# Four layer programs of a graph network joined into one, with weights split at each boundary and the undirected scores computed in strips

## The reference

```python
for layer in (undirected, attention1, attention2, directed):
    h = relu(layernorm(x)); x = x + layer(h)
# undirected, twice:
m_left, m_right = h @ Wl.T, h @ Wr.T
u_left, u_right = h @ m_left.T / sqrt(384), h @ m_right.T / sqrt(384)
u = u_left * (upper triangle and diagonal of adj) + u_right * (upper triangle of adj).T
e = exp(u) * adj; a = e / (e.sum(2) + 1e-10)
h = relu(layer_norm(a @ (h @ Wlin.T + b)) * gain + beta)
# attention
s = q @ k.T * scale + bias; p = softmax(s); out = (p @ v) @ Wo.T + bo
# directed, twice: softmax(h @ h.T / sqrt(384)) * adj, normalised, then three products
# (above, on and below the diagonal) with three weight matrices, layer norm, relu
```

## Time and profile before

| | |
|---|---|
| median of 3 runs | 3056.74 us (3055.41 to 3057.33) |
| the profiled execution | 3056.15 us |
| its span in the trace | 3054.4 us |
| mean granted TensorE clock | 0.983 |
| TensorE busy | 2807.4 us (92%) |
| VectorE, POOL, ScalarE busy | 2043.4 (67%), 1311.5 (43%), 1214.8 us (40%) |

### The profile page before, as it was taken

The page is one execution under the profiler, slowest core; times in us unless marked ns, Lnnn a source line. Parts: engine busy times, 40 slices in busy tenths (PEclk is TensorE's granted clock), DMA queues, the critical chain, the costliest instruction groups (busy, mean ns, idle before and its releaser), DMA issues. The chain is left out here.

```text
span 3054.4 us, 82121 instructions
## 1 busy us (share of the span) xinstructions
PE 2807.4 (92%) x32768; PEld 2576.5 (84%) x32768; DVE 2043.4 (67%) x3932; ACT 1214.8 (40%) x1941; POOL 1311.5 (43%) x2315
## 2 busy tenths in 40 slices
PE   6999999999968999999879999999699999999997
PEld 6888888888868888888768888888588888888886
DVE  4666666666656777777657777777567777777776
ACT  3333333333333333333333333333345454545443
POOL 1212222221213333333323333333267878878787
PEclk9999999999989999999989999999799999999999
DMA  4111111111121111111121111111211111112120
GB/s 137 39 63 50 57 57 57 57 38 61 52 84 37 45 45 45 45 45 45 45 66 46 44 45 44 45 44 47 77 32 46 52 52 52 52 35 68 34 69 31
DMA packets 116482, 158.81 MB, mean 52 GB/s; under 512 B 8000, under 2 KB 112320, under 8 KB 116416
## 3 DMA queue, kind: packets, MB, share of 16 engines
q1 hardware_dynamic: 116416, 157.88, 16.0%
HBM read 107.52 MB, written 50.33 MB: 52 GB/s over the span
## 5 line engine op out<-in xcount | busy, mean ns | idle before, releaser
L162 PE MATMUL ps<-t_hi,w_hi 128*128 128x256 f32 x2304 | 662.7, 288 | 51.7 <-DVE t_lo L900 49.1
L164 PE MATMUL ps<-t_hi,w_lo 128*128 128x256 f32 x2304 | 647.8, 281 | 0.0
L163 PE MATMUL ps<-t_lo,w_hi 128*128 128x256 f32 x2304 | 647.1, 281 | 0.0
L162 PE MATMUL ps<-w_hi,t_hi 128*128 128x384 f32 x1536 | 534.9, 348 | 3.7 <-ACT q L845 3.6
L164 PE MATMUL ps<-w_hi,t_lo 128*128 128x384 f32 x1536 | 517.7, 337 | 0.0
L163 PE MATMUL ps<-w_lo,t_hi 128*128 128x384 f32 x1536 | 517.6, 337 | 0.0
L162 PEld LDWEIGHTS ps<-t_hi,w_hi 128*128 128x128 f32 x2304 | 436.7, 190 | 83.2 <-DVE t_lo L900 58.2
L163 PEld LDWEIGHTS ps<-t_lo,w_hi 128*128 128x128 f32 x2304 | 437.0, 190 | 0.0
L164 PEld LDWEIGHTS ps<-t_hi,w_lo 128*128 128x128 f32 x2304 | 436.7, 190 | 0.0
L814 POOL TENSOR_TENSOR e<-e,factor 128x512 f32<-128x512 f32 x192 | 195.1, 1043 | 448.6 <-DVE factor L938 448.6
L1196 POOL TENSOR_TENSOR hw<-hw,w_row 128x192 f32<-128x192 f32 x512 | 348.1, 711 | 53.8 <-ACT hw L1277 52.3
(11 more groups left out here) (150 smaller groups left out, 6272.9 us busy)
## 6 DMA issues: line engine op xcount, KB each, us to landing
x_after<-xout SPq DMA_DIRECT2D x96, 384.0 KB, 2.5
xin<-x_after SPq DMA_DIRECT2D x96, 384.0 KB, 3.4
xin<-in_x SPq DMA_DIRECT2D x32, 384.0 KB, 4.2
x<-in_x SPq DMA_DIRECT2D x32, 384.0 KB, 3.6
x<-x_after SPq DMA_DIRECT2D x32, 384.0 KB, 3.6
out<-xout SPq DMA_DIRECT2D x32, 384.0 KB, 2.8
w_raw<-in_w SPq DMA_DIRECT2D x4, 2304.0 KB, 8.8
adjin<-in_adj SPq DMA_DIRECT2D x32, 256.0 KB, 3.7
```

What stands on the lines that cost most here:

```text
L162: nc.tensor.matmul(out, lhs_hi, rhs_hi, start=(k == 0), stop=False)
L163: nc.tensor.matmul(out, lhs_hi, rhs_lo, start=False, stop=False)
L164: last = nc.tensor.matmul(out, lhs_lo, rhs_hi, start=False, stop=(k == len(terms) - 1))
```

## The change

There is now one program for all four phases, without a barrier between them. `run` issues, on each engine, the first round of phase 0, then for each phase its round 1 and its loop (`run_middle`), and between two phases a line of the new table `BETWEEN` (`run_between`), in which primed stages are the last ones of the old phase, unprimed stages the first ones of the new, and `w2` is the split of matrix 2. Waits count on the old phase's semaphores where a buffer was used by it.

```diff
+SLOTS = ((0, 1, 2, 3, 4, 5), (0, 1, 2, 3), (4, 5, 0, 1), (2, 3, 4, 5, 0, 1))
+PRESPLIT = {1: (), 2: (0, 1), 3: (0, 1)}
+BETWEEN = [
...
+        "aT_0.1' z_0.1' ml_1.0' hT_1.1' mr_1.0' soft_1.0' aT_1.0' ml_1.1' mr_1.1' z_1.0' soft_1.1' aT_1.1' "
+        "z_1.1' w0 w1 w2 w3 norm.0 hT.0 q.0 norm.1 k.0 hT.1 q.1",
...
+        "stat.0 pv.0' hT.0 soft.1' out.0' stat.1 fac.1' w2 w3 v.0 pv.1' hT.1 soft.0 out.1' fac.0 v.1",
...
+        "pv.0' soft.1' out.0' fac.1' pv.1' out.1' w2 w3 w4 w5 stat.0 stat.1 split_0.0 soft_0.0 att_0.0 "
...
+def run_between(line, ended, begun):
+    for word in line.split():
+        if word[0] == "w" and word[1:].isdigit():
+            begun["weights"](int(word[1:]))
+            continue
+        stage, s = word.rstrip("'").rsplit(".", 1)
+        if word.endswith("'"):
+            ended[stage](int(s), ITER - 1)
+        else:
+            begun[stage](int(s), 0)
...
+def weights_free(eng, phases, phase, m):
+    for past in (phase - 1, phase - 2):
+        if past >= 0 and SLOTS[phase][m] in SLOTS[past]:
+            user = phases[past].weight_users[SLOTS[past].index(SLOTS[phase][m])]
+            for s in range(STREAMS):
+                eng.wait_ge(phases[past].pe_done[s], phases[past].PE[s](user, ITER - 1))
+            return
...
+        def run(eng, k, weights=None):
...
+            run_first(phases[0].orders[k], todo[0])
+            for n, ph in enumerate(phases):
+                def meanwhile(to=n + 1):
+                    if weights:
+                        for m in PRESPLIT[to]:
+                            weights(to, m)
+                run_middle(eng, ph.orders[k], todo[n], meanwhile if n + 1 < len(phases) else None)
+                if n + 1 < len(phases):
+                    run_between(BETWEEN[n][k], todo[n], todo[n + 1])
+            run_last(phases[-1].orders[k], todo[-1])
```

```diff
-                                at = t * P + half * NODES
-                                mm = nc.tensor.matmul(
-                                    b.ps[t * NODES:(t + 1) * NODES, 2 - 2 * l, half * P:(half + 1) * P],
-                                    b.hT[:, c, at:at + NODES], b.mlr[:, c, :, at:at + NODES],
-                                    start=(c == 0), stop=(c == C - 1))
+                            for blk in range(2):
+                                first_token = t * P + half * NODES + blk * HD
+                                to = t * NODES + blk * HD
+                                wanted = slice(blk * HD, blk * HD + 3 * HD)
+                                mm = nc.tensor.matmul(
+                                    b.ps[to:to + HD, 2 - 2 * l, half * P:(half + 1) * P][:, wanted],
+                                    b.hT[:, c, first_token:first_token + HD],
+                                    b.mlr[:, c * T * 2 + t * 2 + half].rearrange("p k j -> p (k j)")[:, wanted],
+                                    start=(c == 0), stop=(c == C - 1), tile_position=(0, to))
```

## The result

The changed kernel took 3013.07 us (median of 4 runs, 3009.77 to 3014.13) against 3057.03 for the kernel before on the same chip: ratio 0.9854 [0.9838, 0.987], 44 us less. The forecast was 3017 in 2998 to 3038.

What follows compares the result with a forecast made beforehand. TensorE's work was taken to bound the phases, the wait that ends last the boundaries. Terms -19.5 + 0 - 20.4 - 8.4 + 8 + 1 = -39.3 from 3056.15 gave 3017 us, range 2998 to 3038.

Steps and rivals of the forecast that it cites:

- boundary 2 to 3: Between phases 2 and 3: first idle time stays, TensorE's second, 6.43 us, goes with 2.5 of clock; -8.4 us (-12 to -5).
- boundary 1 to 2: Between phases 1 and 2: of 32.6 us over the steady distances, 12.2 remain; -20.4 us (-16 to -26.5).
- the two presplits: After round 1 of phases 1 and 2: early splits delay VectorE's softmax and POOL's products; +8 us for both (0 to +12).
- the start: Phase 0's matrices 4 and 5 load some 5 us later, first used in the second layer; +1 us (0 to 2).
- boundary 0 to 1: Between phases 0 and 1: barrier (3.0) and slow POOL pair (1.9) out, four splits (5.2) in; 0 us (-1 to +2).
- The strips: Scores `u` of phase 0: 96 instead of 128 columns, stage 1.53 to 1.225 us, 64 stages; -19.5 us.
- Downstream waits are counted from `u`'s end, so the gain stays: Step of the strips term in phase 0: the whole 0.305 us per stage is kept, 64 times, -19.5 us.
- The load rule: Skill's rule for `u`: loads overlap matmuls only in another row group, so 24 extra loads are exposed; prediction took them as hidden.
- The rival of two strips abreast: Rival for `u`: only two strips run abreast, 24 rounds of 96 columns, stage 2.2 us, +43, kernel 3079 us; chance 0.06.
- The wait at `v`: Boundary 1 to 2: `v`'s product waits for VectorE's splits `w2 w3`, 6.0 us.
- The clock behind it: Boundary 1 to 2: after the idle piece at `v` TensorE's clock falls, costing 2.5 us.
- The 3.7 for the fetch at the loop's end: Boundary 1 to 2: the fetch at the end of the loop remains, 1.91 us plus 1.8 of clock.

Runs made afterwards that it cites:

- e4: The changed kernel with score strips of 32 rows and only 32 columns, three of four score blocks left out: 3015.65 us, 0.9867.
- e2: The changed kernel with the scores as before, whole 64-row blocks of 128 columns, so the seams alone: 3026.96 us, 0.9903.
- e1: The kernel before with the strips and the new element order inside `mlr` alone, boundaries untouched: 3039.74 us, 0.9944.
- e10: The kernel before with 96 unused bytes per partition behind the raw weights, no instruction changed: 3069.06 us, 1.0034.
- e12: The changed kernel with 96 unused bytes per partition behind the raw weights: 3018.23 us, 0.9872.
- e3: The changed kernel with strips of 32 rows but all 128 columns, the unwanted quarter computed too: 3024.35 us, 0.9896.
- e5: The changed kernel with boundary 1 to 2's splits apart, one ahead of the old stream's last product, one behind `v.0`: 3002.72 us, 0.982.
- e11: The changed kernel with all four seam reorderings, VectorE also waiting for POOL's products before each single split in attention rounds: 2970.26 us, 0.9717.

## Why the prediction was right, point by point

- **The sum**: -39.3 forecast, 44 by the medians and 42.2 by the profiled executions. It is closer than its terms. Phase 0 came out 4.0 us worse than forecast and boundary 2 to 3 1.0 worse; boundary 1 to 2 was 2.5 better, phase 3 2.1, the two presplits together 1.8, the start 0.9 and boundary 0 to 1 0.6. That these cancel is luck.
- **The strips**: the mechanism held and the stage's size too (1.20 us measured). The term of -19.5 was mis-sized, at -15.5, in the step "Downstream waits are counted from `u`'s end, so the gain stays". Against the kernel before, `u` takes 20.7 us less between the first and last transposes and `agg` 1.4 less, the products 0.6 less, the transposes 0.7 more, and idle time 6.5 more. This idle time is the step that failed: between 40 and 820 us the waits grew from 28.3 to 32.4, at `agg` and at the attention's transposes, which wait for VectorE, and VectorE's own queue does not get shorter. e4 shows the same with more force.
- **The pace of the products**: nobody forecast it. It makes what the strips gave depend on the kernel that they are set against. Against e2, with the same buffer addresses, the phase kept 9.9 us: idle time is 6.0 longer and the products take 6.7 longer. In e1 it kept 13.7, and there the products' 6.5 us are nearly all that is missing. Between e10 and e12, which have no fast stretch and products of 617.6 and 618.2 us, it kept 19.4, the size of the forecast. That the addresses have a part in the pace is shown by e10 and e12; what turns it from pass to pass, and why e1 has no fast stretch, is open.
- **The load rule**: 48 loads of 110 ns, 5.3 us end to end, stand inside a stage of 1.20 us, all on the same 128 rows of the array. So they overlap matmuls and one another. The Trainium skill, page "TensorE: Matmul & The Clock Gate", section "The mechanism", says in its list of what overlaps that a load overlaps running matmuls only where its row group differs; these rows contradict that "only". (The section itself also names a load into the background weight buffer; no run here shows whether that is at work.) Whether the different column strips let the loads overlap is not shown: the products on the whole array do it too (loads 6.10 us and matmuls 6.07 us of the 6.10 us window above). The rival of two strips abreast fell by the stage's time, 1.20 us where it needed 2.2, and by e3, 1.52 us for twice the matmuls.
- **Boundary 0 to 1**: 0 forecast, -0.6 measured, through the very trade of the forecast: barrier and slow POOL pair out, four splits in.
- **Boundary 1 to 2**: -22.9 for -20.4. The wait at `v` was 6.22 us for 6.0, and e5 took it out. The clock behind it cost 5.9 us for 18 products that take 3.1 at full clock, 2.8 for 2.5. The 3.7 for the fetch at the loop's end is the step that was off: over four steady distances (76.4) only 86.1 - 76.4 = 9.7 are left, of which wait and clock are 9.0. The stall is still there, in the row below, but 1.10 us long instead of 1.91, and no lower clock follows it, where the forecast had 1.8 for that. It is not hidden: it delays the scores, VectorE's softmax starts 0.9 us later than in a steady round (3.54 - 2.63), and the splits and `v` behind it follow. That is about the 0.7 us that are left. That the stall is a fetch of instructions is not shown; the profile names no cause.

```profile
1498.65 0.70 PE L1059 MATMUL ps<-wide 32*64 32x64 f32 x39 [1.10 <-issue]
```

- **Boundary 2 to 3**: -7.4 for -8.4; the 6.43 us idle time and its clock went, the first idle time stayed.
- **Presplits**: +2.4 and +3.8 for +4 each. POOL's late products were the path, as said (2.28 us). The Trainium skill, page "SBUF — State Buffer", section "SBUF: two separate sides", says that the two engines exclude each other for a whole instruction in this case; the trace agrees, with one product beside each split at 2.1 us instead of 1.04, six in all, and e11 with all 192 at 1.04 once no split runs beside them.

## What to carry to other kernels

Removing a barrier gives back only what does not stand behind the next item in an engine's queue: here three seams still held 40 us after it, and moving the splits and the first stages into the old phase's end took them. Work taken off the busiest engine is worth its time only as far as the next engine's queue runs ahead of it; read the waits downstream of the shortened stage before counting its gain whole. Before explaining a difference of a few us, add up the unchanged instructions in both traces: a number that fits the theory, as in e1, can have another cause.

## What the hardware showed that I had not expected

Back-to-back matmuls of the same shape at the same granted clock have two paces, about 113.5 and 117.5 to 120 ns for 128x256, mostly held for a whole stretch. The addresses of the buffers have a part in it: 96 unused bytes per partition cost 12 us of 3057 and 5 of 3013. Yet the same instructions on the same buffers change pace from one pass of a loop to the next. Narrow strips of the array's columns run four abreast with their weight loads hidden: a stage of 48 records takes 1.52, 1.20 and 0.63 us for 128, 96 and 32 columns. And an idle time of TensorE of only 2.12 us was followed by the lower clock and 54 products in 8.16 us, while one of 2.13 us in the next iteration was not, and they took 6.63 (e4).
